# Masked queries and keys: one ScalarE eviction and two strided transfers per tile

## The chip, the cores and the metric

One core of a Trainium2 chip. The metric is the device time of one execution in microseconds; 598.75 us is the median of three executions of the kernel before the change (597.21 to 599.16).

## The reference

A small image tokenizer makes 5 tokens per image, 77 text tokens are put behind them, and 64 sequences of T = 82 tokens with 256 channels go through one attention block and one block of low-rank experts (top 2 of 8). The part that matters here is the attention, with 16 heads of 16 channels and a learned bias by relative position:

```
xn  = (x - mean) * rsqrt(var + eps) * ln_g + ln_b
q, k, v = split(xn @ w_qkv + b_qkv)          # 16 heads, hd = 16
scores = (q @ k.T) / sqrt(hd)
bias[i, j, h] = sinusoid(i - j) @ w_rel[:, h]
attn = softmax(scores + bias)
out  = (attn @ v) @ w_out + b_out
```

All of it is in float32.

## The kernel before

The program has three stages on one core: the tokenizer (about the first 115 us), the attention over 64 sequences, one "batch" b each (117 to 462 us by the scores' first and last matmul), and the experts. Each engine has its own list of instructions in a fixed order, written as loops over b in `attention_and_experts`; semaphores tie the lists together.

*Queries and keys.* Four batches form a quarter group q (16 of them; 4T = 328 tokens). For each q there are four pieces j: two halves of the query channels (j = 0, 1) and two of the key channels (2, 3). `qk(q, j)` on TensorE multiplies the normalised tokens hT by the weights into one of four PSUM banks. The relative position is put into the product itself: of each block of 32 partitions, 16 hold a head's channels and the other 16 hold sines and cosines (for queries) or their products with w_rel (for keys). Heads are woven, so that even partitions belong to the one head (a = 0) and odd ones to the other (a = 1). Each piece is therefore stored twice in the tiles qT and kT (the space is called qk_space in the profile): in copy a, the partitions of head a carry the channels plus bias, the others the position rows. `read_qk(q, j)` on VectorE does it with two passes over all 128 partitions, one per copy:

```
out[:, a] = piece * own[:, a] + add[:, a]     # own: 1 (or 1/sqrt(hd)) on head a's partitions, else 0
```

The tiles have two places (q even, q odd), so the position rows of a place are the same in every group.

*The loop, batch b.* TensorE: `scores(b)` (L1443, 16 products in four PSUM banks, each stored by two records of the profile), `weigh(b-2)` (L1464), four `turn(b-1, g)` (L1452, transposes of the probabilities) and between them the transposes, values and projections that fall due, and `qk` of the next group (L1418). In batch b it is piece j = (b+1) mod 4 of group (b+1)//4 + 1: the last piece, j = 3, of group q is multiplied in batch 4q-2, and the group's first scores are those of batch 4q. VectorE: `shift(b, 0)` and `shift(b, 1)` (maximum L1846, subtraction L1848), in even batches between them `invert` (L1863), then statistics, `read_qk` (L1834), and in odd batches `divide` (L1874). ScalarE: `copy_sums(b-2)` (L1665, from `weigh`), four `copy_probT(b-1, g)` (L1685), between them two `exponent(b, half)` (L1677), copies of what else TensorE made, and, for 16 of the batches, `split` (L1693) at the end. scores(b) wait for the shifts of batch b-1 (their banks) and for the last piece of their group.

*The queue of SP.* SP issues nearly all transfers, in program order, and waits on semaphores in that order. In even batches: `pack` (L1147, early<-early, 64 partitions of 1312 bytes), `send_shares` (L1155), `load_values`, `send_values`, `store`, `spread_shares` (L1164). In odd ones: `gather_den` (L1142) and the same loads and stores. At the end of a batch comes `load(b)`: in batches 19 to 28 tokens (L1103), in batches 25 to 40 the weights of one expert (L1122, 320 KB; wa in odd batches, wb in even ones). Batches 56 and 58 end with `turn_pair` (L1137), two transposing transfers each.

*PSUM banks.* `uses` lists in which order the ring of four banks is taken; `free` makes TensorE wait until the use four places earlier has been read: by VectorE for qk (psQ_dve), by ScalarE for most others (psQ_act). `by_dve` and `by_act` count these reads.

Of the kernel before, what the change touches and what calls it, by code (L numbers as in the profile page):

```python
# [11 lines left out]
ALU = mybir.AluOpType  # L12
# [4 lines left out]
C = 256  # L17
# [17 lines left out]
NFRONT = 22  # L35
NEARLY = 2
QLEAD = 2

# [18 lines left out]
def tokenizer_block(nc, ctx, S, I, R, A, L, big, pout, cout, ident_all, banks):  # L57
    NN = NTOK // 128 * TOPK
    HB = NB // 2
    GROUPS = ((0, 1), (1, 2), (2, 4), (4, 9), (9, 13), (13, 18))  # L60


# [35 lines left out]
    bq_row = early[:, 1024:1024 + C]  # L98
    gbq_row = sb("gbq_row", [128, C])
    pj_row = sb("pj_row", [128, C]); gpj_row = sb("gpj_row", [HB, C])  # L100
    cls = sb("cls", [128, C])
# [31 lines left out]
    def sync(sp):  # L133
        sp.dma_start(patches[:, 0, 0:QLEAD, :], I["patches"][:, 0, 0:QLEAD, :]).then_inc(S["lead_in"], 16)
        for k, (lo, hi) in enumerate(GROUPS):
# [15 lines left out]
            if k == 0:  # L151
                sp.dma_start(patches[:, 0, QLEAD:5, :], I["patches"][:, 0, QLEAD:5, :]).then_inc(S["img_in0"], 16)
            else:
                sp.dma_start(patches[:, lo:hi, :, :], I["patches"][:, lo:hi, :, :]).then_inc(S["img_in%d" % k], 16)
        sp.dma_start(wqkv[:], I["at_w_qkv"].rearrange("(c p) n -> p c n", p=128)).then_inc(S["wqkv_in"], 16)
# [103 lines left out]
    def tensor(te):  # L259
# [5 lines left out]
        def conv(n):  # L265
# [6 lines left out]
            for k, (lo, hi) in enumerate(GROUPS):  # L272
                if n == lo and n > 0:
                    te.wait_ge(S["img_in%d" % k], 16)
            if n >= 2:
# [3 lines left out]
            for q in range(5):  # L279
                if n == 0 and q == QLEAD:  # L280
                    te.wait_ge(S["conv_in"], 16)
                    te.wait_ge(S["img_in0"], 16)
                mm = te.matmul(PS8[n % 2][:, 0:C], patches[:, n, q, :], cwT[:, q, :], start=(q == 0), stop=(q == 4))  # L283
# [325 lines left out]
    def vector(v):  # L609
# [252 lines left out]
        for n in range(11, 22):  # L862
# [16 lines left out]
            if n == 15:  # L879
# [4 lines left out]
                global_weigh(0)  # L884
                v.wait_ge(S["a_step"], 1)
                for a in range(2):
                    v.tensor_scalar(A["bown"][:, a, 0:2], cols[:, 20:22], A["ownq"][:, a:a + 1], None, ALU.mult)
                    ins = v.tensor_scalar(A["bown"][:, a, 2:4], cols[:, 22:24], A["own"][:, a:a + 1], None, ALU.mult)
# [26 lines left out]

    return (sync, gpsimd, tensor, scalar, vector), {"early": early, "cwT": cwT, "wq": wq, "wkv": wkv, "gwq": gwq}

# [31 lines left out]
def attention_space(sb):  # L949
# [4 lines left out]
         "qrel": sb("qrel", [128, 2, T]), "kt0": sb("kt0", [128, 2, T]), "kt1": sb("kt1", [128, 2, T]),  # L954
         "wrel": sb("wrel", [128, 2, 2, 2]), "own": sb("own", [128, 2]), "ownq": sb("ownq", [128, 2]), "bown": sb("bown", [128, 2, 4]),
         "qadd": sb("qadd", [128, 2, 2, T]), "kadd": sb("kadd", [128, 2, 2, T]),
# [12 lines left out]
def attention_and_experts(nc, ctx, S, I, R, A, L, W, H, pc, ident_all, out, banks, old):  # L969
# [47 lines left out]
    place = {use: k for k, use in enumerate(uses)}  # L1017
    to_act = ("xT", "val", "project")
    by_act = {use: 1 + sum(u[0] in to_act for u in uses[:k]) for k, use in enumerate(uses) if use[0] in to_act}
    by_dve = {use: 1 + sum(u[0] == "qk" for u in uses[:k]) for k, use in enumerate(uses) if use[0] == "qk"}  # L1020

# [54 lines left out]
    psH = psS.rearrange("p (a h) n -> p a h n", a=2)  # L1076
    texp = R["tile_expert"]

    def yg(n, k):
# [17 lines left out]
    def sync(sp):  # L1097
# [59 lines left out]
        def spread_shares(m):  # L1157
# [29 lines left out]

        for b in range(-1, NB):
            if b >= 4 and b % 2 == 0:
                pack(b // 2 - 2)  # L1190
# [42 lines left out]
        for n in range(0, NX, 2):  # L1233
            sp.dma_start(yg_two(n), rows[:, n:n + 2, :, :]).then_inc(S["yg_in%d" % (n // 2)], 16)
        for n in range(0, NX, 2):
# [133 lines left out]
    def tensor(te):  # L1369
        def free(use):  # L1370

            k = place[use]
            if k >= RING:
                before = uses[k - RING]
                if before[0] == "weigh":
                    te.wait_ge(S["sums_copied"], before[1] + 1)
                elif before[0] == "qk":
                    te.wait_ge(S["psQ_dve"], by_dve[before])
# [262 lines left out]
    def scalar(act):  # L1641
        def copy_xT(n):
# [3 lines left out]
            if gone >= 0:  # L1646
# [3 lines left out]
                           ACT.Copy).then_inc(S["psQ_act"], 1)  # L1650

        def copy_val(n):

# [102 lines left out]
        for b in range(NB):  # L1756
# [50 lines left out]
        for n in range(NX):  # L1807
            if n % 2 == 0:
                act.wait_ge(S["yg_in%d" % (n // 2)], 16)
            act.activation(yg(n, 1), yg(n, 1), ACT.Copy,  # L1810
                           scale=R["weight"][:, 2 * n + 1:2 * n + 2]).then_inc(S["second_weighed"], 1)

    def vector(v):
# [148 lines left out]
        for b in range(NB):  # L1962
# [42 lines left out]
        for n in range(0, NX, 2):  # L2005
            v.wait_ge(S["yg_in%d" % (n // 2)], 16)
            for k in range(n, n + 2):
# [180 lines left out]
```

## Time and profile before

| | us |
|---|---|
| median of three executions | 598.75 |
| profiled execution | 601.78 |
| its span, first to last instruction | 599.8 |
| TensorE busy (matmul) | 552.0 |
| VectorE busy | 477.0 |
| ScalarE busy | 368.0 |
| GpSimd busy | 315.6 |

All numbers but the first come from one profiled execution. A row of the profile names the line of the kernel, the engine, what is written and read, and the shape. PE is TensorE, PEld its weight loads, DVE VectorE, ACT ScalarE, POOL GpSimd, SP the engine that issues transfers; SPq is SP's issuing itself. A busy matmul is drawn with a modelled end, so a wait shorter than a matmul's tail can be hidden in busy time. `<-` behind an idle time names what ended it. A group of instructions gives its count x, then busy us and mean ns of one, then the engine's idle us ahead of them and what ended it; a row of a timeline gives start and length in us, and in brackets the idle time ahead of it. A landing is counted from the issue on the queue to the last update of the transfer's semaphore.

### The profile page before, as it was taken

The numbers are of one execution on the slowest core, as the hardware profiler recorded it, in microseconds if no ns is written. First come the engines' busy times: TensorE is split into PE (matmuls) and PEld (weight loads), VectorE is DVE, ScalarE is ACT, GpSimd is POOL, SyncE is SP. The second block draws the span as 40 slices with busy tenths as digits, with TensorE's granted clock in tenths as the row PEclk, the third lists the DMA queues.
The fourth block names the chain that finished last, engine by engine and source line by source line (L and its number), as shares of the span: only waits on it lengthen the run. The fifth ranks groups of instructions, "written<-read, shape, count | busy, mean of one in ns | idle before, by whom it ended". The sixth has DMA issues, their size and how long they took to land.

```text
span 599.8 us, 20410 instructions
## 1 busy us (share of the span) xinstructions
PE 552.0 (92%) x7904; PEld 461.8 (77%) x7904; DVE 477.0 (80%) x967; ACT 368.0 (61%) x793; POOL 315.6 (53%) x401
## 2 busy tenths in 40 slices
PE   9999989989999999999999999999997999999940
PEld 8788867767788778877888878888875788888830
DVE  3665858899989999999999998998886666666617
ACT  1222234167667667777778767777777667777724
POOL 1577673437637688888888434442111334444430
PEclk9998999999999999999999999999999699999985
DMA  8999101422232335656766643333453255544239
GB/s 297 398 342 340 53 9 37 141 94 87 79 98 92 112 117 169 188 171 202 213 189 208 192 138 117 103 117 105 129 139 106 69 122 110 116 115 117 73 127 336
DMA packets 78186, 89.49 MB, mean 149 GB/s; under 512 B 33551, under 2 KB 58639, under 8 KB 77581
## 3 DMA queue, kind: packets, MB, share of 16 engines
q1 hardware_dynamic: 73340, 78.20, 43.0%
q0 software_dynamic: 4464, 9.35, 5.0%
q8 instruction: 64, 1.05, 0.8%
q10 hardware_dynamic: 288, 0.66, 0.3%
q14 instruction: 30, 0.24, 0.2%
HBM read 48.82 MB, written 36.29 MB: 142 GB/s over the span
## 4 chain that ended last, share of the span: by engine, by line
PE 58%; DVE 21%; issue 9%; DMA 5%; SPq 3%; ACT 3%; POOL 1%; DVEq 0%; POOLq 0%; ACTq 0%
DVE mx L1846 7%; PE banks L1562 7%; PE banks L1452 7%; PE banks L1418 6%; PE banks L1577 6%; PE banks L283 5%; PE banks L1464 4%; PE banks L1476 4%; PE banks L1430 3%; DVE prob L1848 3%; PE banks L323 3%; DVE qk_space L1834 3%; PE banks L331 2%; PE banks L1547 2%; PE banks L1443 2%
## 5 line engine op out<-in xcount | busy, mean ns | idle before, releaser
L1685 ACT ACTIVATE probT<-banks 82x328 f32<-82x328 f32 x256 | 109.3, 433 | 10.3 <-PE banks L1452 9.9
L1452 PE MATMUL banks<-ident_all,prob 82*82 82x82 f32 x1024 | 111.1, 240 | 0.0
L1848 DVE TENSOR_TENSOR prob<-banks,mx 82x656 f32<-82x656 f32 x128 | 107.1, 837 | 4.4
L1452 PEld LDWEIGHTS banks<-ident_all,prob 82*82 82x82 f32 x1024 | 89.3, 122 | 27.4 <-issue 6.0
L1846 DVE TENSOR_REDUCE mx<-banks 82x8 f32<-82x656 f32 x128 | 104.2, 814 | 4.3 <-PE banks L1443 3.3
L1677 ACT ACTIVATE prob<-prob 82x656 f32<-82x656 f32 x128 | 95.5, 746 | 17.3 <-DVE prob L1848 16.2
L1418 PE MATMUL banks<-hT,wqkv 128*128 128x328 f32 (+10 forms) x320 | 80.5, 385 | 0.0
L1296 POOL TENSOR_TENSOR big<-big,gwq 128x256 f32<-128x256 f32 x41 | 30.3, 741 | 92.4 <-ACT gwq L1672 92.0
L1357 POOL DMA_INDIRECT entry_rows<-cwT,slot_entry x39 | 39.7, 1018 | 63.2 <-ACT cwT L1730 57.4
L1665 ACT ACTIVATE early<-banks 128x328 f32<-128x328 f32 x64 | 28.5, 445 | 58.1 <-PE banks L1464 46.3
L1892 DVE COPY qk_space<-ex_weights 64x640 f32 x78 | 40.7, 522 | 25.7 <-PE banks L1590 25.0
L1443 PE MATMUL banks<-qk_space 32*82 32x82 f32 x2048 | 53.0, 240 | 8.7 <-DVE prob L1848 7.2
L1464 PE MATMUL banks<-probT,vv 82*32 82x82 f32 x2048 | 51.2, 241 | 7.5 <-ACT probT L1685 6.9
L1443 PEld LDWEIGHTS banks<-qk_space 32*82 32x82 f32 x2048 | 43.8, 147 | 17.3 <-issue 10.5
L1418 PEld LDWEIGHTS banks<-hT,wqkv 128*128 128x128 f32 x320 | 50.2, 191 | 7.7
L1721 ACT ACTIVATE hT<-banks 128x1024 f32<-128x1024 f32 (+1 forms) x40 | 38.1, 1000 | 21.2 <-PE banks L1562 21.2
L1464 PEld LDWEIGHTS banks<-probT,vv 82*32 82x32 f32 x2048 | 38.7, 112 | 15.7 <-ACT probT L1685 12.4
L1283 POOL TENSOR_SCALAR xh<-big,a_mv,a_rst 128x256 f32<-128x256 f32 x35 | 45.1, 1289 | 5.9 <-PE banks L1409 2.3
L1476 PE MATMUL banks<-wout,wkv 128*128 128x256 f32 x164 | 44.6, 397 | 0.9 <-DVE wkv L1874 0.8
L1430 PE MATMUL banks<-wqkv,hT 128*128 128x256 f32 x164 | 42.7, 383 | 0.0
L1562 PE MATMUL banks<-wq,qk_space 64*128 64x128 f32 x624 | 42.3, 283 | 0.0
L1562 PEld LDWEIGHTS banks<-wq,qk_space 64*128 64x128 f32 x624 | 38.9, 193 | 3.9 <-issue 3.9
(275 smaller groups left out, 1017.4 us busy)
## 6 DMA issues: line engine op xcount, KB each, us to landing
vv<-value_rows SPq DMA_DIRECT2D x57, 192.0 KB
value_rows<-vs SPq DMA_DIRECT2D x41, 256.0 KB, 2.8
share<-shares SPq DMA_DIRECT2D x64, 82.0 KB
slot_rows<-xh SPq DMA_DIRECT2D x1, 4992.0 KB, 34.0
fused_rows<-in_txt SPq DMA_DIRECT2D x1, 4928.0 KB, 20.6
big<-in_patches SPq DMA_DIRECT2D x2, 1600.0 KB, 11.7
out<-big SPq DMA_DIRECT2D x25, 128.0 KB, 3.1
big<-entry_rows SPq DMA_DIRECT2D x6, 512.0 KB, 6.8
```

What stands on the lines that cost most here:

```text
L1283: pool.tensor_scalar(xh[:, n % 3, :], H[:, n, :], mv[:, n % 4, 0:1], rst[:, n % 4:n % 4 + 1], ALU.subtract, ALU.mult).then_inc(S["xh_ready ...
L1418: mm = te.matmul(bank(("qk", 4 * q + j))[:, lo:lo + size], wqkv[:, c, 128 * j:128 * j + 128], hT[:, c, a:a + size], start=(c == 0), stop=( ...
L1430: mm = te.matmul(bank(("val", n))[:, 0:C], hT[:, c, a:a + 128], wv[:, c, :], start=(c == 0), stop=(c == 1))
L1443: mm = te.matmul(psS[0:T, g, s:s + T], qT[rows, par, a, t, cols], kT[rows, par, a, t, cols], start=True, stop=True)
L1452: mm = te.transpose(bank(("turn", 4 * b + g))[0:T, s * T:s * T + T], prob[:, b % 2, g, s, :], ident_all[0:T, 0:T])
L1464: mm = te.matmul(bank(("weigh", b))[32 * g:32 * g + 32, lo:lo + T], vv[0:T, b % 4, 8 * t + 2 * g + a, :], probT[:, b % 2, g, 2 * t + a, :] ...
L1476: mm = te.matmul(bank(("project", n))[:, 0:C], attT[:, c, a:a + 128], wout[:, c, :], start=(c == 0), stop=(c == 1))
L1562: mm = te.matmul(psH[:, f // 4, h, f % 4 * 128:f % 4 * 128 + 128], wb[rows, p % 2, f * 128:f * 128 + 128], t1T[rows, p % 2, :], start=True ...
L1677: act.activation(prob[:, b % 2, 2 * half:2 * half + 2, :, :], prob[:, b % 2, 2 * half:2 * half + 2, :, :], ACT.Exp).then_inc(S["prob_ready ...
L1685: act.activation(probT[:, b % 2, g, :, :].rearrange("p s t -> p (s t)"), bank(("turn", 4 * b + g))[0:T, 0:4 * T], ACT.Copy).then_inc(S["pr ...
L1846: v.tensor_reduce(mx[:, half, :, :], s4, X, ALU.max).then_inc(S["max_ready"], 1)
L1848: v.tensor_tensor(prob[:, b % 2, 2 * half:2 * half + 2, :, :], s4, mx[:, half, :, :].unsqueeze(3).to_broadcast([T, 2, 4, T]), ALU.subtract ...
```

## The change

For the groups q >= QMOVED = 2 the two VectorE passes are replaced. `copy_qk(q, j)` on ScalarE evicts the piece once from PSUM into one of four row buffers (`rows_qk`, one per j, laid over tiles of the tokenizer that are no longer used), with scale 1/sqrt(hd) for queries and the bias per partition (`qkb`) in the same instruction; it stands at the end of the batch, after the fourth `copy_probT` and ahead of `split`. `send_qk(q, j)` on SP, at the start of the next batch, waits for it and issues two transfers that write the even partitions into copy 0 and the odd ones into copy 1 of qT or kT. The position rows are not written again: the groups 0 and 1, which VectorE still makes, have left them in both places. scores(b) of a moved group wait for the eight transfers of the group (`qk_sent0/1`). The banks of moved pieces are freed by ScalarE. For the first piece of a group SP also waits until the scores that read the place are done, and ScalarE until the transfers of the group before have landed, since the row buffers are single. The other edits rename semaphores so that one is used for two loads that lie far apart, join two bias rows in one tile, and compute `qkb` once in the tokenizer with two small VectorE instructions.

```
...
+    QMOVED = 2
+
+    def to_act(use):
+        return use[0] in ("xT", "val", "project") or (use[0] == "qk" and use[1] >= 4 * QMOVED)
...
+    def moved(b):
+        q = (b + 1) // 4 + 1
+        return [(q, (b + 1) % 4)] if QMOVED <= q < NQ else []
...
+    rows_qk = [old["red"][:].rearrange("p r c -> p (r c)")[:, 0:QT], old["wg1"][:].rearrange("p r c -> p (r c)")[:, 0:QT],
+               old["past"][:].rearrange("p j e -> p (j e)")[:, 0:QT], old["bias_rows"][:].rearrange("p r c -> p (r c)")[:, 0:QT]]
...
+        def send_qk(q, j):
+
+            sp.wait_ge(S["psQ_act"], by_act["qk", 4 * q + j])
+            if j == 0:
+                sp.wait_ge(S["scores_done"], 4 * (q - 1))
+            rows, t = qT if j < 2 else kT, j % 2
+            for a in range(2):
+                sp.dma_start(rows[a:128:2, q % 2, a, t, :], rows_qk[j][a:128:2, :]).then_inc(S["qk_sent%d" % (q % 2)], 16)
...
         for b in range(-1, NB):
+            for q, j in moved(b - 1):
+                send_qk(q, j)
...
         def scores(b):
 
-            te.wait_ge(S["psQ_dve"], by_dve["qk", 4 * (b // 4) + 3])
+            if b // 4 < QMOVED:
+                te.wait_ge(S["psQ_dve"], by_dve["qk", 4 * (b // 4) + 3])
+            else:
+                te.wait_ge(S["qk_sent%d" % (b // 4 % 2)], 16 * 8 * (b // 8))
...
+        def copy_qk(q, j):
+
+            act.wait_ge(S["qk_done"], 4 * q + j + 1)
+            if j == 0 and q > QMOVED:
+                act.wait_ge(S["qk_sent%d" % ((q - 1) % 2)], 16 * 8 * ((q - 1) // 2))
+            act.activation(rows_qk[j], bank(("qk", 4 * q + j))[:, 0:QT], ACT.Identity, bias=A["qkb"][:, j:j + 1],
+                           scale=float(HD) ** -0.5 if j < 2 else 1.0).then_inc(S["psQ_act"], 1)
...
             if b >= 1:
                 copy_probT(b - 1, 3)
+            for q, j in moved(b):
+                copy_qk(q, j)
             for n in projected(b - 5):
                 if n < NX:
                     split(n)
...
-            if (b + 1) // 4 + 1 < NQ:
+            if (b + 1) // 4 + 1 < QMOVED:
                 read_qk((b + 1) // 4 + 1, (b + 1) % 4)
...
```

How the order moves at three places. ScalarE, batch 26, from its last projection's copy to the next batch's copy of the sums (lines of the changed kernel are some 40 higher; L1685 and L1724 are copy_probT, L1677 and L1716 exponent, L1693 and L1732 split, L1665 and L1704 copy_sums). Before:

```order
L1672 ACTIVATE gwq<-banks 128x256
L1685 ACTIVATE probT<-banks 82x328
L1677 ACTIVATE prob<-prob 82x656
L1685 ACTIVATE probT<-banks 82x328
L1693 ACTIVATE cwT<-wq 128x512
L1665 ACTIVATE early<-banks 128x4x82
```

Now:

```order
L1711 ACTIVATE gwq<-banks 128x256
L1724 ACTIVATE probT<-banks 82x328
L1716 ACTIVATE prob<-prob 82x656
L1724 ACTIVATE probT<-banks 82x328
L1688 ACTIVATE bias_rows<-banks,qkb 128x328
L1732 ACTIVATE cwT<-wq 128x512
L1704 ACTIVATE early<-banks 128x4x82
```

The eviction (L1688, here of piece j = 3, whose row buffer lies over bias_rows) has come between the fourth copy_probT and split.

SP, end of batch 26 and start of batch 27 (L1122 and L1139 are the expert weights, L1142 and L1159 gather_den, L1191 send_qk). Before:

```order
L1164 DMA share<-shares 64x1x328 [waits attT_ready,rden_out]
L1164 DMA share<-shares 64x1x328
L1103 DMA big<-fused_rows 128x2x256 [waits h_late0]
L1122 DMA ex_weights<-in_wb 128x640
L1142 DMA den<-early 64x1x41 [waits sums_copied]
L1179 DMA vv<-value_rows 80x512 [waits weigh_done,vals_sent1]
```

Now:

```order
L1181 DMA share<-shares 64x1x328 [waits attT_ready,rden_out]
L1181 DMA share<-shares 64x1x328
L1120 DMA big<-fused_rows 128x2x256 [waits h_late0]
L1139 DMA ex_weights<-in_wb 128x640
L1191 DMA qk_space<-bias_rows 64x328 [waits psQ_act]
L1191 DMA qk_space<-bias_rows 64x328
L1159 DMA den<-early 64x1x41 [waits sums_copied]
L1205 DMA vv<-value_rows 80x512 [waits weigh_done,vals_sent1]
```

The two transfers of piece j = 3 stand directly behind the load of weights and ahead of gather_den; scores(28) wait for them.

SP, end of batch 58 and start of batch 59 (L1137 and L1154 are turn_pair). Before:

```order
L1164 DMA share<-shares 64x1x328 [waits attT_ready,rden_out]
L1164 DMA share<-shares 64x1x328
L1137 DMA_TRANSPOSE cwT<-slot_rows 128x4x128 [waits fx_sent1,fx_sent0]
L1137 DMA_TRANSPOSE cwT<-slot_rows 128x4x128
L1142 DMA den<-early 64x1x41 [waits sums_copied]
L1179 DMA vv<-value_rows 96x512 [waits weigh_done,vals_sent2]
```

Now:

```order
L1181 DMA share<-shares 64x1x328 [waits attT_ready,rden_out]
L1181 DMA share<-shares 64x1x328
L1154 DMA_TRANSPOSE cwT<-slot_rows 128x4x128 [waits fx_sent1,fx_sent0]
L1154 DMA_TRANSPOSE cwT<-slot_rows 128x4x128
L1191 DMA qk_space<-bias_rows 64x328 [waits psQ_act]
L1191 DMA qk_space<-bias_rows 64x328
L1159 DMA den<-early 64x1x41 [waits sums_copied]
L1205 DMA vv<-value_rows 96x512 [waits weigh_done,vals_sent2]
```

The last two transfers of the last group stand behind the transposes; scores(60) wait for them, and gather_den comes after them.

## Rows read from the trace of the kernel before

**Rows 1.** The page, the chain that ended last: span by engine.

```profile
PE 58%; DVE 21%; issue 9%; DMA 5%; SPq 3%; ACT 3%; POOL 1%; DVEq 0%; POOLq 0%; ACTq 0%
```

**Rows 2.** Busy by stretch: length, PE, PEld, DVE, ACT, POOL, clock, DMA.

```profile
135.00:445.00 310.00, 301.71 (x5229) 249.47 (x5222) 287.11 (x517) 224.12 (x524) 193.38 (x254) 1.00 0.47 141
```

**Rows 3.** Waits, 135 to 445 us: us in total, times, longest.

```profile
PE banks L1464 <- ACT probT L1685: 4.2, 20, 0.4
PE banks L1443 <- DVE prob L1848: 3.0, 6, 0.8
...
DVE qk_space L1834 <- PE banks L1418: 14.5, 23, 1.6
```

**Rows 4.** Groups by line, DVE, 135 to 445 us (key pass).

```profile
L1834 DVE SCALAR_TENSOR_TENSOR qk_space<-banks,own,kadd 128x328 f32<-128x328 f32 x57 | 29.0, 550 | 7.8 <-PE banks L1418 7.7
```

**Rows 5.** Groups by line, ACT: L1665 of 135 to 445 us.

```profile
L1665 ACT ACTIVATE early<-banks 128x328 f32<-128x328 f32 x57 | 25.4, 445 | 51.2 <-PE banks L1464 41.9 <-DVE wkv L1874 9.4
...
L1693 ACT ACTIVATE cwT<-wq 128x512 uint16<-128x512 uint16 x16 | 9.9, 620 | 0.0
...
L602 ACT ACTIVATE qadd<-qrel,bown 128x82 f32<-128x82 f32 x4 | 1.4, 352 | 0.0
```

**Rows 6.** The line L1147 (SP, packing), and SP's longest wait.

```profile
L1147 SPq DMA_DIRECT2D early<-early x32: 517/527/1673, 139.0 to 482.5; - x32
...
DMA to landing us min/median/max: 1.9/2.3/4.5
...
SPq L1155 <- DVE den L1863: 73.2, 30, 5.5
```

**Rows 7.** Timeline of SP, 308 to 310 us; landing of its last row.

```profile
308.13 0.49 SPq L1122 DMA_DIRECT2D ex_weights<-in_wa  x1
309.30 0.53 SPq L1147 DMA_DIRECT2D early<-early  x1
...
DMA to landing us min/median/max: 4.5/4.5/4.5
```

**Rows 8.** Expert weight loads (first, last of four); landing of all 16.

```profile
272.56 1.03 SPq L1122 DMA_DIRECT2D ex_weights<-in_wb  x1
...
336.86 0.80 SPq L1122 DMA_DIRECT2D ex_weights<-in_wb  x1
...
DMA to landing us min/median/max: 4.1/4.9/5.7
```

**Rows 9.** Timeline of PE: scores of batches 28 and 40.

```profile
276.57 0.83 PE L1443 MATMUL banks<-qk_space 32*82 32x82 f32 x32
...
340.69 0.83 PE L1443 MATMUL banks<-qk_space 32*82 32x82 f32 x32
```

**Rows 10.** Timelines of ACT, SP and PE around batches 51 and 52.

```profile
399.15 0.42 ACT L1685 ACTIVATE probT<-banks 82x328 f32<-82x328 f32 x1
...
399.08 1.17 SPq L1164 DMA_DIRECT2D share<-shares  x2
...
403.87 0.83 PE L1443 MATMUL banks<-qk_space 32*82 32x82 f32 x32
```

**Rows 11.** Timelines of SP, PE and DVE near the loop's end.

```profile
442.59 3.35 SPq L1137 DMA_TRANSPOSE cwT<-slot_rows  x2
445.99 0.58 SPq L1142 DMA_DIRECT2D den<-early  x1
...
445.31 0.83 PE L1443 MATMUL banks<-qk_space 32*82 32x82 f32 x32
...
457.66 0.57 DVE L1874 TENSOR_TENSOR wkv<-early,share 128x32 f32<-128x32 f32 x2 [3.34 <-DMA share<-shares]
```

**Rows 12.** Timeline of PE at two waits, and the stretch of 0.50 clock.

```profile
129.04 0.83 PE L1443 MATMUL banks<-qk_space 32*82 32x82 f32 x32 [1.02 <-DVE prob L1848]
...
461.88 0.83 PE L1443 MATMUL banks<-qk_space 32*82 32x82 f32 x32 [1.89 <-DVE prob L1848]
...
462.90:476.60 13.70, 12.75 (x132) 10.74 (x134) 11.30 (x18) 8.91 (x17) 4.81 (x5) 0.50 0.25 73
```

More of the change, by code:

```diff
@@ L36 @@
 NEARLY = 2
+GROUPS = ((0, 1), (1, 2), (2, 4), (4, 9), (9, 13), (13, 18))
 QLEAD = 2
@@ L98, in tokenizer_block @@
     bq_row = early[:, 1024:1024 + C]
-    gbq_row = sb("gbq_row", [128, C])
-    pj_row = sb("pj_row", [128, C]); gpj_row = sb("gpj_row", [HB, C])
+    bias_rows = sb("bias_rows", [128, 2, C])
+    gbq_row, pj_row = (bias_rows[:, k, :] for k in range(2))
+    gpj_row = sb("gpj_row", [HB, C])
     cls = sb("cls", [128, C])
@@ L273, in conv @@
                 if n == lo and n > 0:
[L274 removed]
+                    te.wait_ge(S["piece_in%d" % k], 16)
             if n >= 2:
@@ L885, in vector @@
                 v.wait_ge(S["a_step"], 1)
+                v.tensor_scalar(A["qkb"][:, 0:2], cols[:, 20:22], float(HD) ** -0.5, None, ALU.mult)
+                v.tensor_copy(A["qkb"][:, 2:4], cols[:, 22:24])
                 for a in range(2):
@@ L914, in vector @@
             read_quarter(k)
-    return (sync, gpsimd, tensor, scalar, vector), {"early": early, "cwT": cwT, "wq": wq, "wkv": wkv, "gwq": gwq}
+    return (sync, gpsimd, tensor, scalar, vector), {"early": early, "cwT": cwT, "wq": wq, "wkv": wkv, "gwq": gwq, "red": red, "wg1": wg1, "past": past, "bias_rows": bias_rows}
 LATE = ("agg", "aggT", "loutT", "lout", "wpj", "wmod", "gwkv", "gwpj", "gv", "mod_row", "gbv_row", "cls_row", "bkv_row", "xn", "xT", "qv",
@@ L954, in attention_space @@
          "qrel": sb("qrel", [128, 2, T]), "kt0": sb("kt0", [128, 2, T]), "kt1": sb("kt1", [128, 2, T]),
-         "wrel": sb("wrel", [128, 2, 2, 2]), "own": sb("own", [128, 2]), "ownq": sb("ownq", [128, 2]), "bown": sb("bown", [128, 2, 4]),
+         "wrel": sb("wrel", [128, 2, 2, 2]), "own": sb("own", [128, 2]), "ownq": sb("ownq", [128, 2]), "bown": sb("bown", [128, 2, 4]), "qkb": sb("qkb", [128, 4]),
          "qadd": sb("qadd", [128, 2, 2, T]), "kadd": sb("kadd", [128, 2, 2, T]),
@@ L1017, in attention_and_experts, with to_dve @@
     place = {use: k for k, use in enumerate(uses)}
-    to_act = ("xT", "val", "project")
-    by_act = {use: 1 + sum(u[0] in to_act for u in uses[:k]) for k, use in enumerate(uses) if use[0] in to_act}
-    by_dve = {use: 1 + sum(u[0] == "qk" for u in uses[:k]) for k, use in enumerate(uses) if use[0] == "qk"}
+    QMOVED = 2
+    def to_act(use):
+        return use[0] in ("xT", "val", "project") or (use[0] == "qk" and use[1] >= 4 * QMOVED)
+    def to_dve(use):
+        return use[0] == "qk" and use[1] < 4 * QMOVED
+    by_act = {use: 1 + sum(to_act(u) for u in uses[:k]) for k, use in enumerate(uses) if to_act(use)}
+    by_dve = {use: 1 + sum(to_dve(u) for u in uses[:k]) for k, use in enumerate(uses) if to_dve(use)}
+    def moved(b):
+        q = (b + 1) // 4 + 1
+        return [(q, (b + 1) % 4)] if QMOVED <= q < NQ else []
     def sb(name, shape, dt=F32):
@@ L1077, in attention_and_experts, with rows_in @@
     texp = R["tile_expert"]
+    def rows_in(k):
+        return 16 + 16 * (k < len(GROUPS))
     def yg(n, k):
@@ L1233, in sync @@
         for n in range(0, NX, 2):
-            sp.dma_start(yg_two(n), rows[:, n:n + 2, :, :]).then_inc(S["yg_in%d" % (n // 2)], 16)
+            sp.dma_start(yg_two(n), rows[:, n:n + 2, :, :]).then_inc(S["piece_in%d" % (n // 2)], 16)
         for n in range(0, NX, 2):
@@ L1376, in free @@
                     te.wait_ge(S["sums_copied"], before[1] + 1)
-                elif before[0] == "qk":
+                elif before in by_dve:
                     te.wait_ge(S["psQ_dve"], by_dve[before])
```

11 lines of the change are left out of this document (5 added, 6 removed).

## The prediction

> **What bounds the kernel now.** I read the chain of waits first, then busy time by stretch, then the waits of each engine, then single transfers. The chain that ended last lies 58% on TensorE and 21% on VectorE [rows 1]: read it as two engines of almost equal length that hand the lead to each other. The change acts only in the attention loop, 64 batches from 117 to 462 us, so I look at 135 to 445 us alone. There TensorE is busy 301.71 of 310 us and VectorE 287.11 [rows 2]: VectorE is nearly full, but TensorE is fuller. So whatever VectorE loses, the loop can win only what TensorE waits, and that is small: 8.3 us idle, of which 4.2 us wait for ScalarE's copies of the turned probabilities (late because the exponential before them waited for VectorE) and 3.0 us for VectorE itself [rows 3]. A matmul's end is modelled, so a short wait can hide behind a "busy" tail; I let the true figure lie between 6 and 13 us. A batch takes 310/57 = 5.4 us (57 copies of sums lie in the stretch [rows 5]).
>
> **The change, part by part.**
>
> *VectorE's two passes go.* 56 pieces (14 quarter groups q = 2 to 15, four pieces each) times two passes of 550 ns [rows 4] are 61.6 us off VectorE, about 1.1 us a batch, and with them its waits for the qk matmul, 14.5 us [rows 3]. VectorE then ends each batch about a microsecond before TensorE, and nearly all of TensorE's waits for it should go. Gain: between 6 and 13 us; I take 9, a little over the 8.3 us that are shown as idle. Not more, because the weigh matmuls stand close behind ScalarE's copies in any case.
>
> *ScalarE's copy comes.* 56 copies of 128x328 from PSUM. The nearest row is the copy of the sums, the same shape, 445 ns [rows 5]; with a bias per partition it may be longer (the 128x82 Identity with such a bias takes 352 ns [rows 5], too much for 82 columns), so 0.45 to 0.65 us, I take 0.5. It stands after the fourth probT copy of a batch, exactly where ScalarE idles before the copy of the sums: 51.2 us in 57 batches, 0.9 us each [rows 5]. So it costs nothing, unless the split for the experts (16 batches) stands there too; then 0.5 + 0.6 us [rows 5] exceed the 0.9 by 0.2, in 16 batches 0 to 3 us. I take 0.5. The bank of the piece comes free about when VectorE freed it before.
>
> *Two transfers per piece come on SP's queue.* 112 issues at 0.53 us [rows 6] are 59 us of SP. SP waits 73.2 us for VectorE's reciprocal alone [rows 6], so its order, not its sum, is what counts. Each transfer is 64 partitions of 1312 bytes, the same as the packing of the sums (early<-early), which lands after 1.9 to 4.5 us, median 2.3 [rows 6].
>
> *TensorE's wait moves from a VectorE instruction to a landing.* scores(4q) needs all eight transfers of its group. The last pair (j = 3) leaves ScalarE at the end of batch 4q-2 and is wanted at the start of batch 4q, about 4.3 us after the last probT copy. An undisturbed case is batch 50: that copy ends at 399.57, ours would end at 400.1; SP is busy with the shares until 400.25, issues our pair until 401.4, and the second lands 2.3 us after its issue at 400.85, at 403.15; scores(52) start at 403.87 [rows 10]. Margin 0.7 us. Shorter batches eat a few tenths of it. Nine such groups: 0 to 3 us, I take 0.5.
>
> *Four groups sit behind a weight load.* In batches 25 to 40 SP ends each batch with a load of 320 KB for the experts; at 26, 30, 34 and 38 that load is directly ahead of our last pair. A transfer behind such a load does not land in 2.3 us: the packing issued at 309.30, 1.2 us after a load, took 4.5 us, until 313.8 [rows 7]. By the Trainium skill, page "DMA: Bandwidth & Descriptors", section "Anatomy of one DMA", a DMA costs about 2.0 us plus its bytes at 436 GB/s, an estimate of 2.2 us for our 82 KB whatever is ahead; that fits the median but not the packing behind the load, and by it these four would be on time and the sum 6 us better. The measurement decides. The load of batch 26 is issued at 272.56, that of batch 38 at 336.86, and the 16 loads land after 4.1 to 5.7 us, median 4.9 [rows 8]; our pair follows 0.4 us later. So it lands at 277.9 and 342.2, where scores(28) and scores(40) start at 276.57 and 340.69 [rows 9]: 1.3 and 1.5 us late. Four times 1.4 is 5.6; with the loads at 4.1 us it is 2.4, at 5.7 us 8.8. TensorE being the bound, it is lost in full. With scores wanted a little earlier I take 6.
>
> *The end of the loop.* In batch 58 SP issues two transposes, 442.59 to 445.94, and the last pair of the last group comes behind them; scores(60) started at 445.31 [rows 11]. Ours lands at 446.6 + 2.3 = 448.9, 3.6 us late. Part of it is swallowed, since VectorE waits 3.34 us for the shares three batches on, at 457.66 [rows 11]. But that wait hangs on SP too, and SP now issues the pair (1.2 us) ahead of the gather of the denominators at 445.99. So 1.2 to 5 us (the upper end if nothing is swallowed and the clock follows); I take 2.5.
>
> **Sum:** -9 + 0.5 + 0.5 + 6 + 2.5 = +0.5 us. The profiled execution took 601.78 us (span 599.8), so 602.3 by it; it is 3.0 us over the median of the runs shown, 598.75, so by the median 599.2. About 0.3% (1.8 us) is what a measurement of this kernel can tell from no change; my forecast is **no change that can be told**, 599.5 us (rounded up, as the open ends are longer on the slow side). Its own range, from the bounds above, is 594 to 605.
>
> **Rivals.**
>
> *The transfers keep up.* For it: the median landing of 2.3 us and the margin of 0.7 us, and a pair is quick work. Against: the order on SP at four groups. If the loads land at their 4.1 us and the tail costs its least, -11 + 0 + 2.4 + 1.2 = -7.4, some 591.5 us (589 to 596). The rule of the page cited above would make it so at the four groups.
>
> *Waits at scores pull TensorE's clock down* (the slower one). Mechanism: every fourth batch TensorE now stands still for a transfer, at one place, once for 3.6 us. Price: after TensorE had idled from 460.0 to 461.88, the granted clock was 0.50 from 462.9 to 476.6, the 1.2 of the two levels (1.2 and 2.4 GHz) [rows 12]; matmul work takes up to twice as long in it, so such a spell of 13.7 us costs some 5 us. It decides from stops of that length: after one of 1.02 us at 128 us the clock stayed at 1.00 [rows 12]. My stops in the weight stretch, 1.3 to 2 us, lie between the two. One or two spells in mid-loop and one at its end, with transfers landing at their slow end: +0.5 + 3 x 3 to 5, some 605 to 614 us, 609 as its middle. The Trainium skill, "TensorE: Matmul & The Clock Gate", Part 1, says that the slow clock is the default and that activity releases it; the trace agrees with a slow spell after the idle one.
>
> *The change only moves the bound* to ScalarE: it is busy 224.12 of 310 us [rows 2], 252 with the copies. Then TensorE goes on waiting for probT; the gain falls to 3 and the sum to +6.5, 605 us. Its idle time before the sums speaks against it.
>
> **How the numbers follow.** Cancelling (forecast) 0.45, transfers keep up 0.22, clock and late transfers 0.26, ScalarE 0.07. Of the 0.45 I put 0.12 below -0.3%, 0.21 within, 0.12 above; ScalarE's 0.07 goes half to within, half to above. Faster 0.12 + 0.22 = 0.34; same 0.21 + 0.03 = 0.24; slower 0.12 + 0.26 + 0.04 = 0.42. The range has to take in both rivals up to their middles: 590 to 609 us.
>
> **What would show it.** Right: VectorE loses some 60 us of busy time in the loop and no longer appears before scores; in batches 28, 32, 36 and 40 and at 60 scores wait for a DMA into qk_space by 1 to 3.6 us; the other groups wait under 0.3 us; the copy on ScalarE lasts near 0.5 us and its idle time before the sums shrinks by as much; the granted clock stays 1.00 until about 450. Wrong: DMA waits at nearly every fourth batch (then the 2.3 us or SP's free time is off), a clock of 0.50 before 440, or TensorE's waits for probT still near 4 us.

## The result and the profile after

The changed kernel took 621.05 us (median of 4; 618.3 to 624.14), the kernel before beside it 598.95: a ratio of 1.0366 [1.0325, 1.0407], 3.7% slower and outside the range that was given. The profiled execution took 618.3 us with a span of 616.3. Of every run below, the time in us is the median of all its executions, and the ratio leaves out those in a slower state of the chip.

The chain that ended last, by engine, of the kernel after (before: [rows 1]):

```profile
PE 63%; DMA 12%; SPq 8%; DVE 8%; issue 4%; ACT 4%; POOL 1%; DVEq 0%; POOLq 0%; ACTq 0%
```

VectorE's part of the chain has shrunk (21% to 8%), and what came in its place is transfers and their queue: 20% together, where they had 8%. Busy time by stretch, kernel after, columns as in [rows 2]:

```profile
135.00:445.00 310.00, 292.86 (x4943) 242.08 (x4936) 226.88 (x391) 235.72 (x551) 190.44 (x251) 0.97 0.52 162
```

TensorE, busy 301.71 of these 310 us before, now stands still for 17 of them, and its clock is below 1.00. What the engines wait for there (total, times, longest):

```profile
PE banks L1474 <- DMA qk_space<-bias_rows: 14.7, 10, 2.6
PE banks L1495 <- ACT probT L1724: 1.1, 4, 0.4
PE banks L1474 <- DVE prob L1889: 0.9, 2, 0.6
...
DVE mx L1887 <- PE banks L1474: 59.1, 42, 3.9
DVE wkv L1915 <- DMA share<-shares: 12.1, 13, 2.1
```

Against [rows 3]: TensorE's waits for VectorE and for probT fell from 7.2 to 2.0 us, as said. In their place stands a wait of scores (L1474) for the last pair of a group, and VectorE's freed time became idle time ahead of its maxima. With the wait at the loop's end (3.2 us, at 464.68) TensorE stands 17.9 us for transfers in 11 of the 14 moved groups. Four of these stops, from PE's timeline (scores of batches 28, 44, 52 and 60):

```profile
280.83 0.93 PE L1474 MATMUL banks<-qk_space 32*82 32x82 f32 x32 [2.65 <-DMA qk_space<-bias_rows]
...
375.22 0.83 PE L1474 MATMUL banks<-qk_space 32*82 32x82 f32 x32 [2.03 <-DMA qk_space<-bias_rows]
...
420.06 0.83 PE L1474 MATMUL banks<-qk_space 32*82 32x82 f32 x32 [0.96 <-DMA qk_space<-bias_rows]
...
464.68 0.83 PE L1474 MATMUL banks<-qk_space 32*82 32x82 f32 x32 [3.16 <-DMA qk_space<-bias_rows]
```

Batch 28 was forecast to stop (behind a weight load), 60 too (behind the transposes); 44 and 52 were not. SP's timeline ahead of scores(48), where no load is near:

```profile
391.61 0.33 SPq L1205 DMA_DIRECT2D vv<-value_rows  x1
392.04 0.37 SPq L1212 DMA_DIRECT2D out<-big  x1
392.50 1.17 SPq L1181 DMA_DIRECT2D share<-shares  x2
393.79 1.15 SPq L1191 DMA_DIRECT2D qk_space<-bias_rows  x2
394.98 0.59 SPq L1159 DMA_DIRECT2D den<-early  x1
```

SP issues the pair at once (ScalarE's copy ended at 393.77), but the last of it lands at 398.28, 3.9 us after the second issue, where 2.3 had been assumed. The single updates of the semaphores in this trace, counted:

```
transfer                       updates   when (us)
first parts of the pair        22 of 32  395.51 to 396.35
rest of the pair               10 of 32  396.78 to 398.28
two spreads of shares ahead     2 of 10  393.54 and 394.11
the same, rest                  8 of 10  395.83 to 397.69
```

A transfer of the pair gives 16 updates, a spread 5: one about 1.0 us after its issue, and four later. Of the pair's 32, 22 (11 of each transfer) come 1.7 to 2.0 us after their issue, near the packing ahead of them, which took 1.9 us in all (389.91 to 391.82). Ten are late, until 0.6 us behind the last of the spreads ahead. The pair of the last group (q = 15), whose spreads were issued 3.6 us and more ahead of it, has no late one: all 32 have come by 2.0 us after its second issue. That the ten stand behind the work of the spreads is a reading of these counts; the trace does not tell which part went where.

### The profile page after: what moved, and what is told of

It is laid out like the page before. It is cut to its first block, busy times and chain, and to the rows that moved or that the text cites. A ratio compares the mean times of both kernels' runs of the same rounds, so it can differ in the third digit from the quotient of the medians.

```text
span 616.3 us, 20439 instructions
## 1 busy us (share of the span) xinstructions
PE 555.3 (90%) x7904; PEld 465.2 (75%) x7904; DVE 428.7 (70%) x857; ACT 391.4 (64%) x849; POOL 315.1 (51%) x401
## 4 chain that ended last, share of the span: by engine, by line
PE 63%; DMA 12%; SPq 8%; DVE 8%; issue 4%; ACT 4%; POOL 1%; DVEq 0%; POOLq 0%; ACTq 0%
PE banks L1483 7%; DMA qk_space<-bias_rows 7%; PE banks L1593 7%; PE banks L1446 6%; PE banks L1608 5%; PE banks L283 5%; PE banks L1474 5%; PE banks L1495 5%; PE banks L1507 4%; PE banks L1458 4%; PE banks L323 3%; SPq L1191 2%; PE banks L331 2%; DVE mx L1887 2%; PE banks L1578 2%
## 5 line engine op out<-in xcount | busy, mean ns | idle before, releaser
L1724 ACT ACTIVATE probT<-banks 82x328 f32<-82x328 f32 x256 | 110.0, 435 | 13.2 <-PE banks L1483 12.2
L1483 PE MATMUL banks<-ident_all,prob 82*82 82x82 f32 x1024 | 112.4, 242 | 0.5 <-ACT early L1704 0.5
L1716 ACT ACTIVATE prob<-prob 82x656 f32<-82x656 f32 x128 | 95.3, 744 | 9.5 <-DVE prob L1889 9.2
L1474 PE MATMUL banks<-qk_space 32*82 32x82 f32 x2048 | 53.7, 242 | 22.2 <-DMA qk_space<-bias_rows 17.9
L1474 PEld LDWEIGHTS banks<-qk_space 32*82 32x82 f32 x2048 | 44.0, 149 | 31.2 <-DMA qk_space<-bias_rows 19.9
L1933 DVE COPY qk_space<-ex_weights 64x640 f32 x78 | 39.4, 505 | 25.8 <-PE banks L1621 25.0
L1704 ACT ACTIVATE early<-banks 128x328 f32<-128x328 f32 x64 | 28.5, 446 | 42.0 <-PE banks L1495 37.7
L1311 POOL TENSOR_SCALAR xh<-big,a_mv,a_rst 128x256 f32<-128x256 f32 x35 | 43.8, 1252 | 5.9 <-PE banks L1437 2.3
L1507 PE MATMUL banks<-wout,wkv 128*128 128x256 f32 x164 | 46.1, 408 | 0.0
L1458 PE MATMUL banks<-wqkv,hT 128*128 128x256 f32 x164 | 44.1, 392 | 0.0
L283 PE MATMUL banks<-cwT,big 128*128 128x256 f32 x180 | 40.4, 380 | 2.8 <-DMA big<-in_patches 2.2
```

The source lines that it names most:

```text
L1458: mm = te.matmul(bank(("val", n))[:, 0:C], hT[:, c, a:a + 128], wv[:, c, :], start=(c == 0), stop=(c == 1))
L1474: mm = te.matmul(psS[0:T, g, s:s + T], qT[rows, par, a, t, cols], kT[rows, par, a, t, cols], start=True, stop=True)
L1483: mm = te.transpose(bank(("turn", 4 * b + g))[0:T, s * T:s * T + T], prob[:, b % 2, g, s, :], ident_all[0:T, 0:T])
L1507: mm = te.matmul(bank(("project", n))[:, 0:C], attT[:, c, a:a + 128], wout[:, c, :], start=(c == 0), stop=(c == 1))
L1716: act.activation(prob[:, b % 2, 2 * half:2 * half + 2, :, :], prob[:, b % 2, 2 * half:2 * half + 2, :, :], ACT.Exp).then_inc(S["prob_ready ...
L1724: act.activation(probT[:, b % 2, g, :, :].rearrange("p s t -> p (s t)"), bank(("turn", 4 * b + g))[0:T, 0:4 * T], ACT.Copy).then_inc(S["pr ...
```

## The experiments

A ratio is to the kernel before, run beside it (medians 598.9 to 600.4). Three theories of what is lost: **A**, the last pair lands too late for scores; **D**, SP, standing at the batch's head for ScalarE's copy, holds up the chain of shares, which brings the softmax's reciprocal sums to VectorE's division (gather, packing, reciprocal, send, spread, divide); **E**, the transfers hold that chain up by their issues and their load. **B** is A for the groups behind weight loads alone; **C** says that the gain is not there.

**What the passes were worth.** All transfers are left out, and the waits for them; scores read what the first two groups left:

```diff
-            for q, j in moved(b - 1):
-                send_qk(q, j)
...
-                te.wait_ge(S["qk_sent%d" % (b // 4 % 2)], 16 * 8 * (b // 8))
+                te.wait_ge(S["psQ_act"], by_act["qk", 4 * (b // 4) + 3])
...
```

> All 112 transfers into the query and key tiles are left out, with the waits for them (scores wait for ScalarE's copy instead and read what the first two groups left there). It bounds what VectorE's 61.6 us are worth with ScalarE's copies paid. Theories A and B: 590 us (586 to 593), the 9 us that the prediction put down as gain. Theory C: 596 or more.

Measured: 594.38 us, 0.9917 [0.9883, 0.9950], between the theories. The gain of freeing VectorE, ScalarE's copies paid, is 5 us (3 to 7 by the interval), where the prediction had 8.5 (9 less 0.5), though 61.6 us of work went: there TensorE is already busy 305 of 310 us and VectorE idles:

```profile
135.00:445.00 310.00, 305.16 (x5318) 253.03 (x5322) 242.32 (x410) 250.13 (x588) 194.19 (x257) 1.00 0.47 143
```

**One piece of four left on VectorE** (the urgent one, j = 3):

```diff
-        return [(q, (b + 1) % 4)] if QMOVED <= q < NQ else []
+        return [(q, (b + 1) % 4)] if QMOVED <= q < NQ and (b + 1) % 4 < 3 else []
...
```

> Only the pieces j = 0 to 2 are moved; the last piece of a group stays with VectorE's two passes, and scores wait for six transfers. Theory A (the last pair is late because it lands behind the two spreads of shares, everything else of the change pays): no DMA wait at scores is left, VectorE gets 28 passes of 0.55 us back, the clock stays at 1.00 to 450 us, and the time is 594 us (590 to 598). Theory B (only pairs behind weight loads are late): the same 594, so this run does not part A from B. Theory C (the gain is not there, since ScalarE's copy or 84 transfers cost as much as VectorE's passes): 600 us or more.

Measured: 599.93 us, 1.0006 [0.9963, 1.0049]. No wait for a transfer is left at scores, nor at ScalarE, and still nothing is won: theory C's number. If three pieces off VectorE are worth what four are, something besides the urgent pair costs 5 us.

**The last pair elsewhere on SP.** Ahead of the spreads, or only ahead of the loads:

```diff
             for q, j in moved(b - 1):
-                send_qk(q, j)
+                if j < 3:
+                    send_qk(q, j)
...
+            for q, j in moved(b):
+                if j == 3:
+                    send_qk(q, j)
             if b >= 4 and b % 2 == 0:
                 spread_shares(b // 2 - 2)
```

> SP issues the last pair of a group ahead of the two spreads of shares of the same even batch, so also ahead of that batch's load. Theory A: the pair lands 2.0 to 2.5 us after its issue, DMA waits at scores fall from 17.9 us to under 4, the time is 597 us (592 to 603), with the spreads some 2 us later. Theory B: only the four groups behind weight loads get better, by 1 to 2.5 us each; the waits of groups 2, 6, 11 to 13 stay, and the time is 610 to 615.

> SP issues the last pair behind the spreads of shares but ahead of the token and weight loads. Theory A: waits at scores stay in nearly all groups, those of groups 7 to 10 get shorter by 0.5 to 1 us each, 615 to 619 us. Theory B: the waits of groups 7 to 10 vanish and the clock stays up there, 605 to 610 us.

Measured: 613.48 us, 1.0257 [1.0173, 1.0340], and 611.97 us, 1.0178 [1.0113, 1.0242]. Both theories were half right: by its time the first lies where B had it, by its waits where A had it, and the second lies between the two. Ahead of the loads alone 11 us (1.9%) come back, more than A gave: loads do matter. But at the four groups behind weight loads scores still wait; scores of batches 28, 32 and 36 in that run (those of 40 do not wait):

```profile
276.84 0.83 PE L1478 MATMUL banks<-qk_space 32*82 32x82 f32 x32 [1.38 <-DMA qk_space<-bias_rows]
...
300.60 0.83 PE L1478 MATMUL banks<-qk_space 32*82 32x82 f32 x32 [0.60 <-DMA qk_space<-bias_rows]
...
324.62 0.83 PE L1478 MATMUL banks<-qk_space 32*82 32x82 f32 x32 [1.87 <-DMA qk_space<-bias_rows]
```

Ahead of the spreads, the pair lands 3.0 us after its second issue in the mean of the 14 groups (2.0 to 5.2), where it took 3.8 in the change (2.0 to 5.5), and 3.5 us of waits for it at scores are left in three groups, but the spreads are late instead. TensorE's and VectorE's waits of that run, 135 to 445 us:

```profile
PE banks L1487 <- ACT early L1708: 5.5, 8, 1.2
PE banks L1478 <- DVE prob L1893: 4.7, 8, 0.9
PE banks L1499 <- ACT probT L1728: 3.0, 15, 0.4
PE banks L1478 <- DMA qk_space<-bias_rows: 1.3, 2, 0.7
...
DVE wkv L1919 <- DMA share<-shares: 44.6, 22, 3.9
```

The wait at scores went from 14.7 to 1.3 us there, VectorE's wait for shares from 12.1 to 44.6, and TensorE pays through ScalarE and VectorE. Two chains that are due in the same batch share one queue: what the one gains the other loses. Part of the loss is SP standing for ScalarE's copy of the last piece, now ahead of the spreads (12.4 us in 11 waits).

**The transfers alone.** In all four, scores wait for ScalarE's copy instead of the transfers and read what the first two groups left. First the transfers go into a spare tile; then they carry constants into the row buffers, and ScalarE writes aside and waits for none of them (the edit is shown), with and without SP's wait for ScalarE; last come SP's waits without a transfer:

```diff
+            if j == 0 and q > QMOVED:
+                sp.wait_ge(S["qk_sent%d" % ((q - 1) % 2)], 16 * 8 * ((q - 1) // 2))
...
-                sp.dma_start(rows[a:128:2, q % 2, a, t, :], rows_qk[j][a:128:2, :]).then_inc(S["qk_sent%d" % (q % 2)], 16)
+                sp.dma_start(rows_qk[j][a:128:2, :], constant[a:128:2, :]).then_inc(S["qk_sent%d" % (q % 2)], 16)
...
-            act.activation(rows_qk[j], bank(("qk", 4 * q + j))[:, 0:QT], ACT.Identity, bias=A["qkb"][:, j:j + 1],
+            act.activation(aside[:], bank(("qk", 4 * q + j))[:, 0:QT], ACT.Identity, bias=A["qkb"][:, j:j + 1],
...
```

> All 112 transfers are issued at the same places, but write into a spare tile that nobody reads, and scores wait only for ScalarE's copy (they read what the first two groups left). Against the run without transfers (594.4) it gives the price of the transfers alone, with nobody waiting for them. Theory A (only the wait costs): 594 to 596. Theories D and E (SP's order, or the load on the transfer engines, makes the shares late): 599 to 604, with VectorE's waits for shares above 20 us.

> ScalarE writes its copies into a spare tile, the 112 transfers of the same form carry constants into the four row buffers, and no engine but SP ever waits for them (scores wait for ScalarE's copy and read what the first two groups left). SP waits for ScalarE's copies at the batch's head as in the change. Against 594.4 us without transfers. Theory A (only the waits at scores cost): 594 to 596. Theories D and E: 604 to 615, with VectorE's waits for shares above 18 us and TensorE's waits spread over ScalarE and VectorE.

> The same 112 transfers at the same places of SP's list, but SP no longer waits for ScalarE's copy before it issues them; nobody waits for them. Theory D (SP standing at the batch's head for ScalarE holds up the gather and the packing): 594 to 597. Theory E (issues and load on the transfer engines): 602 to 612.

> No transfers; SP only waits for ScalarE's copies at the batch's head, as the change does, and then goes on. Theory D: 600 to 608. Theory E: 594 to 596, as without transfers.

Measured, in this order: 615.44 us (1.0267 [1.0217, 1.0317]), 605.44 (1.0070 [1.0032, 1.0108]), 602.13 (1.0023 [0.9988, 1.0058]), 595.25 (0.9921 [0.9896, 0.9946]). The first, slower than all its theories had it, still had ScalarE wait 14.3 us for its row buffers, and TensorE 8.2 us for ScalarE behind that, so it is no clean price; the second comes nearer. SP's waits for ScalarE by themselves cost nothing: D falls as a cause of its own. The transfers cost 1.1% (6.4 us) without SP's wait for ScalarE and 1.5% (9.2 us) with it; the 2.8 between the two lie inside their intervals. E is the theory that is left. But it is not so that nobody waits for these transfers: TensorE, VectorE and ScalarE do not, but SP, once a group and ahead of the packing, waits until those of the group before have landed, which the change does not do. With SP's wait for ScalarE and without it, 135 to 445 us:

```profile
SPq L1192 <- DMA bias_rows<-kadd: 11.9, 9, 2.2
```

```profile
SPq L1191 <- DMA bias_rows<-kadd: 12.5, 9, 2.5
```

So 6.4 and 9.2 us have this wait in them, and the transfers by themselves may cost less. What speaks for E without it is the run with the last piece on VectorE: there no engine and no queue waits for a landing of the pairs, and its ratio is 0.9% above that without transfers, with intervals that do not meet. Whether issues or load make the price was not separated; issuing the pairs from another engine's queue, which would do it, was not tried. VectorE's wait for shares, 135 to 445 us, without transfers:

```profile
DVE wkv L1911 <- DMA share<-shares: 7.0, 8, 2.7
```

and with the transfers alone (SP waiting for ScalarE):

```profile
DVE wkv L1916 <- DMA share<-shares: 23.6, 15, 3.9
```

Where it begins: the mean time from ScalarE's second copy of sums to SP's issue of the gather, 28 pairs of batches:

```
before 0.42   without transfers 0.33   SP's waits alone 0.38   transfers, SP not waiting for ScalarE 1.59   transfers, SP waiting 1.83 us
```

In odd batches the gather now comes behind a pair that takes SP 1.2 us to issue.

**More slack for the last pair.** Multiplied one batch earlier: with j = 2 in an odd batch (so two pairs stand ahead of the packing, and the edit is shown); the same with the pairs behind gather and packing; and with j = 1, 2 together in an even batch:

```diff
+    def made(b):
...
+        return [(q, 2), (q, 3)] if j == 2 else [(q, j)] if j < 2 else []
```

> The last two pieces of a group are both multiplied in batch 4q-3 and none in 4q-2, so that the last pair leaves a whole batch earlier; all else as in the change. Theory A (the time is lost because the last pair has no slack): no DMA wait at scores but perhaps one of under 1 us, clock 1.00 up to 445 us, and 598 us (595 to 602), near the 600 of the run with the last piece on VectorE. A rival of it (the pieces' place is not the matter, TensorE would wait for ScalarE or VectorE at the same places instead): 608 or more. Theory D (pairs at the head of SP's batch hold up packing and the shares behind them, and this costs 5 us): 600 to 603, since two pairs now stand ahead of the packing.

> As the run with two pieces in one batch, and SP issues the pairs behind the gather of the denominators and behind the packing, ahead of the sending of shares, where it waits for VectorE's reciprocal. Theory D: 595 us (592 to 598), 4 to 6 below the run with the pairs at the head. Theory E (it is the load of the transfers, wherever they stand): no better than that run, within 2 us.

> All but one of the groups are multiplied as j = 0, then j = 1 and 2 in one even batch, then j = 3 one batch earlier than in the change, so that the last pair has a batch of slack and the two pairs of one batch are issued in an odd batch, away from the packing. Theory H (what made the other order slow is two pairs ahead of the packing): no wait at scores, 606 us (602 to 611), as the transfers alone. Its rival (two pieces in one batch make TensorE's batch too long for the engines behind it): 615 to 626.

Measured: 625.57 us (1.0470 [1.0386, 1.0555]), 622.93 (1.0436 [1.0370, 1.0502]) and 613.04 (1.0180 [1.0110, 1.0250]). No wait for a transfer of over 0.3 us is left at scores in any of them, and all are slower than the transfers alone; theory A's 598 is missed by 28 us. The first of them, 135 to 445 us:

```profile
PE banks L1481 <- DVE prob L1896: 11.0, 15, 1.3
PE banks L1502 <- ACT probT L1731: 5.0, 19, 0.5
...
DVE wkv L1922 <- DMA share<-shares: 35.6, 20, 4.8
...
SPq L1198 <- ACT bias_rows L1695: 37.5, 11, 4.8
```

Its clock there was 0.99. Two pairs in the packing's batch go with late shares, and VectorE waits for them. SP also stands 37.5 us for ScalarE's copy of the last piece, ahead of the packing, where the change has 0.4. That SP's waits cost nothing was measured for the places that they have in the change, and not for this one. With the pairs behind gather and packing that wait is 18.8 us, and the time hardly better. With the two pieces in an even batch (24.4 us of waiting for shares) the ratio is 2.9% lower, as theory H said; the median lies 2 us above H's range, the ratio inside it (610 us). Whether TensorE's longer batch is the rest was not separated.

**Order within the queue, with three pieces moved**: the pairs behind gather and packing.

> As the run with the last piece on VectorE, with the six remaining transfers of a group issued behind the gather and the packing. Theory D: 595 us (593 to 597) instead of 600, and VectorE's waits for shares fall from 22 us to about 14. Theory E: 599 to 601.

Measured: 603.33 us, 1.0064 [1.0035, 1.0093], no better than with the pairs at the head (1.0006), and VectorE's wait for shares is 20.3 us where it was 18.9. The order alone does not help: for E, against D.

**ScalarE's row buffers.** The profile after shows ScalarE waiting for them:

```profile
ACT red L1688 <- DMA qk_space<-bias_rows: 10.0, 8, 2.2
```

A second buffer for the first piece:

```diff
+        return rows_two[:] if j == 0 and q % 2 else rows_qk[j]
...
-            if j == 0 and q > QMOVED:
+            if j == 1 and q > QMOVED:
```

> The change with a second row buffer for the first piece of a group, so that ScalarE waits for the transfers of the group before one batch later, when they have long landed. Theory G (ScalarE's wait of 10.0 us for row buffers is part of what is lost): 610 to 615 us. If it stands only while TensorE waits for the same landing anyway: 618 to 623, as the change.

Measured: 618.81 us, 1.0336 [1.0275, 1.0397]: as the change, within the intervals. ScalarE's wait is gone and nothing is won, which fits that it stood while TensorE waited for the same landing.

**Fewer pieces.** Queries only (measured twice), and the first piece alone, by the same line as above with `< 2` and `< 1`:

> Only the pieces j = 0, 1 are moved (56 transfers, 31 us off VectorE), neither of them urgent. If gain and cost both shrink with the pieces, between 594 and the 600 of three pieces: 597 us (595 to 600). If any transfer beside the shares costs more than the VectorE pass it replaces: 600 or more.

> The kernel with only the query pieces moved, once more with more rounds: 597 us, 0.3 to 0.8% below the kernel before, if it is a real gain; an interval that holds 1 if it is not.

> Only the first piece of a group is moved (28 transfers, 15.4 us off VectorE). If gain goes with VectorE's passes and cost with the transfers: 597.5 to 599, between the kernel before and that with two pieces moved. If a first transfer costs nothing since the queue has room: 596 to 597, as good as two pieces.

Measured: 597.50 us (0.9948 [0.9911, 0.9985]), 598.03 (0.9964 [0.9936, 0.9992]) and 595.59 us (0.9927 [0.9898, 0.9956]). With one piece, 28 transfers, the kernel is 0.7% faster than before the change; it reaches what all passes gone without any transfer gave (0.9917), and its interval overlaps those of two pieces. Its row for the stretch, and VectorE's wait for shares there:

```profile
135.00:445.00 310.00, 303.39 (x5283) 251.15 (x5281) 278.66 (x493) 231.66 (x542) 192.20 (x255) 1.00 0.48 150
```

```profile
DVE wkv L1916 <- DMA share<-shares: 3.8, 8, 0.8
```

Pieces moved against ratio: 0, 1.0000; 1, 0.9927; 2, 0.9948 and 0.9964; 3, 1.0006; 4, 1.0366.

## Why the prediction was wrong

Put together from the runs' ratios, times 599.5 us: passes gone, copies paid, -5.0; the transfers +6.4; SP's wait for ScalarE on top +2.8; waiting for the landing +17.7 (the change against the transfers alone); in all +21.9. These are differences of ratios, which add up by construction, and the price of the transfers holds the wait of SP that the change lacks. The forecast's terms were -8.5 (gain and copy), nothing for the transfers, and +9.0 for the three landings: 3.5, 9.2 and 8.7 us are missing. That 17.7 lies by the 17.9 us that TensorE stands for transfers in the profile is in part chance: other waits go, and a lower clock comes within it. The bounds of the terms, added one by one, give 589 to 613 us and not the 594 to 605 beside the sum; both end short of 621.

- **Bound.** Right: TensorE is fuller, so 61.6 us off VectorE are worth little. The size was off: 9 less 0.5 for ScalarE's copies taken, 5 measured (3 to 7).
- **ScalarE's copy**: 521 ns where 500 was taken, and covered: ScalarE's idle time ahead of the copies of sums fell from 51.2 to 30.8 us. Right. The rival that ScalarE becomes the bound did not come: TensorE's waits for probT fell to 1.1 us.
- **"Its order, not its sum, is what counts", two transfers per piece at no cost of their own.** This step failed first. SP's 73.2 us of waiting for the reciprocal [rows 6] were read as free room. Between 135 and 445 us that wait was 68.7 us before, 66.9 without transfers, 35.1 with SP's waits alone, and in the change:

```profile
SPq L1172 <- DVE den L1904: 6.3, 11, 1.0
```

The wait belongs to the chain of shares. Before the change VectorE does not wait for shares there at all; with VectorE freed it waits 7.0 us even without transfers, so their chain is due sooner, just when 1.2 us of issues and 164 KB are put into every batch of it. The runs price that at 6 to 9 us, SP's extra wait included.
- **The landing of 2.3 us, for the groups without a load: 0.5 us.** This step failed too, by nearly as much. The figure was read from the packing [rows 6], which SP issues only when the gather has landed, so little is ahead of it. The pair stands behind two spreads, and in many groups a value transfer; in 13 of the 14 groups it took 2.8 to 5.5 us from its second issue, and 2.0 in the last. The waits of the six groups without a weight load that stood (2, 4, 6, 11, 12, 13) sum to 7.3 us. Group 6 stands behind a token load, issued 0.5 us ahead of the pair; the text had looked at weight loads alone.
- **Four groups behind weight loads: 6 us.** Right in place, and in size by its number: 2.65, 2.15, 1.18 and 1.44, together 7.4 us. The number is in part luck. With the pair ahead of the loads the same four still wait 3.9 us, so the load is about half of it, and the rest is what the other groups have too. Nor is a single stop a firm number: the run with the second row buffer, as fast as the change, has 3.05, 1.56, 3.39 and 0.30. The page "DMA: Bandwidth & Descriptors" of the Trainium skill, section "Anatomy of one DMA", gives the figure behind the prediction's 2.2 us for transfers issued by GpSimd, and no term there counts what is ahead. The pairs, issued by SP, landed 2.0 to 5.5 us after their second issue in this trace; "whatever is ahead" was the prediction's own reading.
- **Loop's end: 2.5 us.** Right in place: 3.16 us at scores(60). With the spreads 3.6 us and more ahead of it, this pair landed 2.0 us after its second issue, close to the 2.3 taken. The further price was not isolated.
- **The clock.** The slower rival's mechanism came, in three of four spells smaller than its 3 to 5 us. Two stretches of the kernel after, around and behind a stop of 2.15 us (with the slow spell in it by itself) and behind one of 1.18:

```profile
300.00:313.00 13.00, 10.85 (x116) 9.51 (x115) 8.36 (x17) 7.92 (x18) 11.33 (x15) 0.74 0.63 187
305.40:312.10 6.70, 6.70 (x84) 5.82 (x85) 4.54 (x9) 3.85 (x9) 5.76 (x7) 0.50 0.50 157
...
330.00:337.00 7.00, 6.68 (x156) 5.51 (x157) 4.34 (x6) 5.22 (x13) 5.16 (x6) 1.00 0.59 209
```

The granted clock was 0.50 in the spell, the 1.2 of the two levels (1.2 and 2.4 GHz). A mean of 0.74 over 13 us is 3.4 us at full speed lost; the spells behind the stops of 2.17, 2.65 and 2.03 us (0.91 over 18 us, 0.93 over 24, 0.88 over 14) add some 5. So some 8 us at most, and it is not needed for so slow a time: the run with two pieces in an odd batch had 0.99 and was slower still. The prediction took stops of 1.3 to 2 us to lie between 1.02 us, without a slow spell, and 1.89, with one [rows 12]. The clock behind the first, which is not in those rows, was 1.00:

```profile
115.00:145.00 30.00, 25.11 (x390) 19.30 (x392) 27.80 (x52) 16.59 (x39) 14.60 (x18) 1.00 0.21 67
```

The length of a stop does not settle it by itself: with the pair ahead of the loads the clock stayed at 1.00 behind a stop of 1.57 us (at 161.47) and fell behind one of 1.38 (at 276.84):

```profile
162.00:180.00 18.00, 18.00 (x314) 15.35 (x309) 13.38 (x24) 13.08 (x32) 5.91 (x9) 1.00 0.37 112
277.00:284.00 7.00, 7.00 (x118) 5.75 (x118) 4.63 (x9) 4.37 (x11) 5.95 (x9) 0.76 0.81 260
```

Slower had the largest chance, 0.42, and the slower rival named late transfers; its upper end of 614 us was short by the two failed steps.

## What to carry to other kernels

A landing time read where little is ahead on the queue is too short for one that has neighbours (2.3 us read, up to 5.5 met); read it from the transfer that stands behind the same neighbours, and count what is ahead. Time that a queue spends waiting is not free if the wait belongs to a chain that becomes urgent as soon as the engine ahead of it is relieved. When the bound lies on another engine, relieve only as much as the bound can use: here one pair of passes in four gave as much as all four did without any transfer, and further ones won nothing more.

## What the runs showed of the hardware beyond what was expected

- A spread of shares (64 partitions of 1312 bytes from four broadcast rows) and the gather of the denominators give 5 updates each to their semaphore in the kernel after, the first about 1.0 us after the issue and four later; the pair's transfers (64 partitions of the same length) give 16. Of the pair behind the spreads ahead of scores(48), 22 of 32 came within 2.0 us of their issue and 10 later.
- The copy of 128x328 from PSUM with a bias per partition takes 521 ns, the plain one of the same shape 446. By line, kernel after:

```profile
L1688 ACT ACTIVATE bias_rows<-banks,qkb x14: 509/521/533, 155.3 to 457.5; 128x328 f32<-128x328 f32 x14
```

- In the kernel after, up to 445 us, the granted clock fell behind TensorE's stops of 2.03 to 2.65 us and stayed at 1.00 behind that of 1.18. With the pair ahead of the loads it fell behind one of 1.38 us and stayed at 1.00 behind one of 1.57.
